# The exponential behind the step's copy, and a query prepared one batch ahead: order of events in a batch loop of attention

## The reference

```python
    x = x + _L0_xattn_ref(ctx_1024, _layernorm(x, axis=-1), mask_BxS2_bk0, ...)
    ...
        xn = layer_norm(x, g1, b1)                      # x here: the context, (16, 1601, 256)
        ln_lat = layer_norm(latents, g2, b2)
        q = ln_lat @ Wq
        kv = jnp.concatenate([xn, ln_lat], axis=1) @ Wkv
        ...                                             # 16 heads of 64
        weight = jnp.einsum('bhld,bhnd->bhln', q * scale, k * scale)
        weight = jnp.where(full_mask[:, None, None, :], weight, neg)
        weight = jax.nn.softmax(weight.astype(jnp.float32), axis=-1).astype(q.dtype)
        out = jnp.einsum('bhln,bhnd->bhld', weight, v)
        return out @ Wout
```

## Time and profile before

| | us |
|---|---|
| median of 3 runs | 1907.46 (1906.87 to 1907.48) |
| the profiled execution's own time | 1906.96 |
| its span in the profile | 1905.2 |
| PE busy | 1805.6 (95%) |
| DVE busy | 1339.1 (70%) |
| ACT busy | 953.3 (50%) |
| POOL busy | 597.4 (31%) |

### The profile page before, as it was taken

One profiled execution on the slowest core, in us unless ns is written; L12 is line 12 of the kernel. 1 busy time (PEld: TensorE's weight loads), 2 busy tenths in 40 slices (PEclk: granted clock), 3 DMA queues, 4 the chain that ended last, 5 costly groups with the idle time before them and its releaser, 6 DMA issues. The chain is left out here.

```text
span 1905.2 us, 32021 instructions
## 1 busy us (share of the span) xinstructions
PE 1805.6 (95%) x10259; PEld 1573.4 (83%) x10259; DVE 1339.1 (70%) x3147; ACT 953.3 (50%) x1665; POOL 597.4 (31%) x647
## 2 busy tenths in 40 slices
PE   5889999999999999999999999999999978888998
PEld 4678888888888888888888888888888877766886
DVE  7577767777777777776767777777777437767666
ACT  4545555554645454555555554645454323334444
POOL 3424344241515151524334241515150013430000
PEclk9989999999999999999999999999999999999999
DMA  7812313131313122222313131313131585502231
GB/s 279 292 54 87 107 45 116 40 110 47 103 47 103 64 89 80 79 88 87 108 42 114 41 109 47 103 47 103 64 108 51 199 351 208 205 2 78 91 116 36
DMA packets 125421, 197.24 MB, mean 104 GB/s; under 512 B 71568, under 2 KB 95024, under 8 KB 119216
## 3 DMA queue, kind: packets, MB, share of 16 engines
q1 hardware_dynamic: 125360, 196.45, 30.8%
HBM read 123.01 MB, written 73.42 MB: 103 GB/s over the span
## 5 line engine op out<-in xcount | busy, mean ns | idle before, releaser
L249 PE MATMUL o_bank<-probT,val 128*128 128x512 f32 x2496 | 684.9, 410 | 7.6 <-DVE probT L888 5.0
L249 PE MATMUL s_bank<-late,fore 128*128 128x416 f32 x3072 | 626.0, 353 | 12.5 <-DVE fore L893 10.3
L249 PEld LDWEIGHTS s_bank<-late,fore 128*128 128x128 f32 x3072 | 570.4, 188 | 42.9 <-issue 11.5
L249 PEld LDWEIGHTS o_bank<-probT,val 128*128 128x128 f32 x2496 | 438.7, 189 | 90.2 <-DVE probT L888 11.6
L852 ACT ACTIVATE prob<-prob,negmax 128x1665 f32<-128x1665 f32 x128 | 216.2, 1689 | 379.2 <-DVE negmax L917 379.2
L888 DVE TENSOR_TENSOR probT<-t_bank,probT 128x512 fp32r<-128x512 f32 x416 | 283.0, 687 | 145.7 <-ACT probT L830 140.8
L830 ACT ACTIVATE probT<-t_bank 128x512 fp32r<-128x512 f32 x416 | 242.8, 591 | 222.4 <-PE t_bank L969 222.2
L912 DVE CUSTOM_DVE_ANT_0 prob<-s_bank,bias 128x416 f32<-128x416 f32 x512 | 295.8, 585 | 67.6 <-PE s_bank L249 66.6
L969 PE MATMUL t_bank<-ident,prob 128*128 128x128 f32 x1664 | 251.0, 274 | 10.5 <-DVE probT L888 6.4
L969 PEld LDWEIGHTS t_bank<-ident,prob 128*128 128x128 f32 x1664 | 205.9, 141 | 51.7 <-DVE probT L888 13.9
L806 POOL TENSOR_TENSOR late_y<-w_raw,late_y 128x1280 fp32r<-128x1280 f32 x16 | 48.1, 3007 | 397.3 <-ACT late_y L824 397.3
(11 more groups left out here) (215 smaller groups left out, 1895.9 us busy)
## 6 DMA issues: line engine op xcount, KB each, us to landing
o_scratch<-outT SPq DMA_DIRECT2D x32, 1024.0 KB, 4.8
stage<-in_ctx SPq DMA_DIRECT2D x48, 512.0 KB, 3.9
w_scratch<-late_y SPq DMA_DIRECT2D x16, 1280.0 KB, 6.5
ffn_w<-o_scratch SPq DMA_DIRECT2D x9, 2048.0 KB, 8.9
qk<-qk_scratch SPq DMA_DIRECT2D x16, 1024.0 KB, 6.8
ffn_w<-w_scratch SPq DMA_DIRECT2D x16, 1024.0 KB, 7.2
late_y<-o_scratch SPq DMA_DIRECT2D x6, 2048.0 KB, 8.1
w_raw<-in_wall SPq DMA_DIRECT2D x16, 640.0 KB, 7.0
```

Source lines behind the costliest of these rows:

```text
L249: mm = pe.matmul(out, weights(a), moving(b), start=first and n == 0, stop=last and n == 2)
```

## The change

The diff moves entries in the lists of events, and nothing else is computed. E i no longer follows A i 3 at once: it is put after the T of the same chunk step (behind Q i+1, and behind what scores of the next pair the step has). Where a step has no T (X of batch 0) it is put after the step's scores. Q 0 of a batch leaves the start of X, except in batch 0, and becomes event G at the end of the Y ahead, behind chunk step 11. Only ACT takes part in E; only ACT and DVE in Q and G. So PE's own order stays as it is.

```diff
 X_AT = {"W": 6, "P3": 10, "N0": 3, "N1": 7, "S4": 6, "S0": 10, "S1": 12}
-Y_AT = {"P7": 9, "N2": 0, ...
+Y_AT = {"P7": 9, "G": 11, "N2": 0, ...
...
-        ev += [("K", 0, 0), ("K", 1, 0), ("Q", 0), ("K", 0, 1), ("K", 1, 1)]
+        ev += [("K", 0, 0), ("K", 1, 0)] + ([] if has_b else [("Q", 0)]) + [("K", 0, 1), ("K", 1, 1)]
...
+            done = [("E", i) for i, j in here if j == 3]
+            if not has_b:
+                ev += done
...
             if c + 2 < CH:
                 ev += [("T", 1, c + 2)]
+            if has_a:
+                ev += done
             ev += [("V", 1, c)]
...
         ev += [("T", 0, c + 2)] if c + 2 < CH else [("T", 2, c - 11)]
+        ev += [("E", i) for i, j in here if j == 3]
         ev += [("V", 0, c)]
...
+        if has_next and c == Y_AT["G"]:
+            ev += [("G",)]
...
-    if j == 3:
-        ev += [("E", i)]
...
-            if ("Q", 0) in x and b.off > 0:
+            if ("K", 0, 0) in x and b.off > 0:
                 F.mask_bias(pool, b)
...
-                if kind == "Q":
+                if kind in "QG":
 
-                    i = e[1]
-                    wait(act, q_in, b, 16, 16)
-                    wait(act, score_out, b, 32, 4 * i - 4)
+                    i, n = (e[1], b) if kind == "Q" else (0, Batch(b.off + 1, b.turn))
+                    wait(act, q_in, n, 16, 16)
+                    wait(act, score_out, n, 32, 4 * i - 4)
```

More of the change, by code:

```diff
@@ L71 @@
 X_AT = {"W": 6, "P3": 10, "N0": 3, "N1": 7, "S4": 6, "S0": 10, "S1": 12}
-Y_AT = {"P7": 9, "N2": 0, "N3": 0, "S2": 3, "S3": 3, "H": (3, 3, 5, 6, 8, 9, 10)}
+Y_AT = {"P7": 9, "G": 11, "N2": 0, "N3": 0, "S2": 3, "S3": 3, "H": (3, 3, 5, 6, 8, 9, 10)}
 H_CHUNKS = ((13, 0, 1), (2, 3), (4, 5), (6, 7), (8, 9), (10, 11), (12,))
@@ L90, in plan_x @@
                 ev += [("K", 0, 3), ("K", 1, 3)]
-            for i, j in units[at:at + X_UNITS[c]]:
+            here = units[at:at + X_UNITS[c]]
+            for i, j in here:
                 ev += unit_events(i, j, 0)
             at += X_UNITS[c]
+            done = [("E", i) for i, j in here if j == 3]
+            if not has_b:
+                ev += done
             if c == X_AT["P3"] and has_b:
@@ L127, in plan_y @@
     for c in range(CH):
-        for i, j in units[at:at + Y_UNITS[c]]:
+        here = units[at:at + Y_UNITS[c]]
+        for i, j in here:
             ev += unit_events(i, j, 4)
@@ L889, in half @@
                                       ALU.subtract).then_inc(t_done, 1)
-                if kind == "Q":
-                    i = e[1]
-                    wait(dve, q_high, b, 8, i + 1)
+                if kind in "QG":
+                    i, n = (e[1], b) if kind == "Q" else (0, Batch(b.off + 1, b.turn))
+                    wait(dve, q_high, n, 8, i + 1)
                     dve.tensor_tensor(qkT[:, i % 2, :, 1, :], qk32[:, i, :, :, :].rearrange("p k h l -> p k (h l)"),
```

## The result

The changed kernel takes 1885.55 us (median of 4, 1884.22 to 1886.81) against 1907.47 before (4 runs): a ratio of 0.9885, 95% interval 0.9873 to 0.9896. That is 21.9 us less; 22 were forecast, and the time lies 0.55 us from the predicted 1885.

What follows compares the result with a forecast made beforehand. PE was taken to bound the kernel, idle 1.30 us a batch. Terms 8.5 + 6.45 + 5.8 + 1.0 = 21.75 us, taken from 1906.96, gave 1885.2, predicted as 1885 us, range 1881 to 1891.

Steps and rivals of the forecast that it cites:

- pair 7's exponential: Near the end of Y: the stall before a transposition goes, 0.51 us in 15 batches, more in batch 0, together 8.5 us.
- pairs 2 and 3: X, step 9: the old stall goes, gaining 0.50 less 0.07 charged at chunk 12, in 15 batches: 6.45 us.
- query 0: Turn into a batch: stall for the query's low part shrinks, 5.8 us with POOL first at the port, otherwise 9.25.
- batch 0: In batch 0's X: pair 2's exponential no longer stands ahead of query 4, and work behind comes earlier: 1.0 us.
- The bound and the stake: Batch loop: PE sets the pace, so the most the change can give is its idle time, 1.30 us a batch.
- Rival 1: In X: pair 2's delay comes back, another 0.43 us a batch is lost, 6.45 less gain, 1891.7 us; chance 0.12.
- Rival 3: End of Y: DVE gets the port before POOL, so query 0 gives 9.25 us, sum 1882; chance 0.2.
- Rival 4: The clock falls, ending within 0.2% of no change; place and chance are not in the text given.

Runs made afterwards that it cites:

- The early split: The changed kernel with query 0 split at step 6 of Y instead of step 11: 1880.71 us.
- pair 7's exponential alone: Against the kernel before, only the exponential of pair 7 moved, in all 16 batches; other exponentials and query 0 stay where they were: 1897.34 us.
- the doubled delay: The changed kernel, but pair 2's exponential of batches 1 to 15 one copy later, behind that of chunk 10: 1919.73 us.
- pair 2 as before: The changed kernel, but pair 2's exponential of batches 1 to 15 back at its old place, right behind its scores: 1881.50 us.

## Why the prediction was right

The mechanisms were right, and the total was closer than its terms. Both kernels issue the same instructions on TensorE in the same order, so their starts can be compared one by one; that puts the gain in the batch loop where it belongs:

| term | worked out | measured |
|---|---|---|
| pair 7's exponential | 8.5 | 9.4 |
| pairs 2 and 3 | 6.45 | 6.2 |
| query 0 | 5.8 | 4.0 |
| batch 0 | 1.0 | 2.6 |
| sum | 21.75 | 22.2 |

Query 0 brought 1.8 us less than was worked out, and batch 0 with pair 7 brought 2.5 more. That these errors nearly cancel is luck.

**The bound and the stake.** Read rightly: TensorE sets the pace, 1.30 us idle a batch was the stake, and 1.14 of it came (89.30 to 88.16).

**Pair 7's exponential, 8.5 us.** The stall is gone as reckoned, in all batches: 0.57 us each in 15 of them (0.51 was worked out) and 0.9 in batch 0. Alone the edit gave more, by the race at batch 1 and the clock in batch 0, neither of which is in this term.

**Pairs 2 and 3, 6.45 us.** The old stall went, the new lateness came exactly where it was put, at chunk 12 behind pair 3's scaling. Its size was 0.14 rather than 0.07 us a batch, and moving pair 2 back gave 0.19. The working also missed that query 4's low part would meet the weights' split of GpSimd and take 0.81 instead of 0.42 us; VectorE waits 1.9 us for the exponential soon after, so it cost nothing. The starts of pair 2's exponential and scaling, counted from the transposition of chunk 9, are within 0.02 us of those worked out: that starts at 720.49 after and 731.12 before, the exponential at +1.13 (worked out: 1.12), the scaling at +3.13 (3.12).

**Query 0, 5.8 us.** The query's low part did lose the port to the centring, by 0.07 us where 0.03 was worked out. With a margin that thin the call was luck as much as reckoning. The stall that stays is 0.45 instead of the 0.36 implied (0.13 and 0.23). The early split shows the parts: 0.25 for the port and 0.20 that stays without it. Over the 15 turns that gave 4.0 us: 1.0 and 1.1 at those into batches 1 and 15, 0.15 to 0.18 at the looped ones (0.27 was worked out), and 0.02 at the one into batch 2, where less was to be had than 0.63, because the loss was 0.50 before.

The Trainium skill's rule ("SBUF — State Buffer", section "Who interferes with whom"), that the one issued first holds the port for its whole length, is borne out by both sides of the race: with GpSimd 0.07 us ahead VectorE's 0.41 us became 2.60, with VectorE 0.08 us ahead (batch 1 of pair 7's exponential alone) it took 0.42 and GpSimd's bias 1.68 instead of 1.48.

**Batch 0, 1.0 us.** The term that was mis-sized most in proportion. Only query 4's stall was counted; the shorter wait for pair 3's scaling came on top. TensorE of the kernel before at the loop's first transposition, that of half 0 and the next batch's first scores; the last line is the changed kernel's first scores.

```profile
82.97 1.94 PE L983 MATMUL s_bank<-ident,stage 128*128 128x128 f32 x16 [2.30 <-PEq L1840]
...
115.38 1.68 PE L969 MATMUL t_bank<-ident,prob 128*128 128x128 f32 x8 [4.04 <-DVE prob L924]
...
166.86 1.39 PE L249 MATMUL s_bank<-late,fore 128*128 128x416 f32 x6 [1.23 <-DVE fore L893]
```

```profile
162.96 1.37 PE L257 MATMUL s_bank<-late,fore 128*128 128x416 f32 x6 [0.17 <-issue]
```

The kernel before takes 32.41 us from the first to the second, the changed one 29.83: 2.58 us. Both ran at the lower clock for some 10 us in this batch, and the gain reaches batch 1 in full. All of batch 0 is 4.50 us shorter (83.89 against 79.39): 2.6 by this order, 0.9 by pair 7's stall, 1.0 at the turn.

**Rivals.** Rival 1 (pair 2's delay comes back) was true in kind and small, 2.9 us at most; the doubled delay shows what it would have cost, and that the slower end was only one copy away. Rival 3 (VectorE wins the port) was open until the run, and missed by 0.07 us. Rival 4 (the clock falls) didn't come: it stayed at 1.00 in the looped batches. Its size was also mis-stated: 21.75 us are 1.5% of the 1432 us of the loop, not 1.2%.

## What to carry to other kernels

An engine that takes part in many short chains should not let a long instruction without urgency stand ahead of a short one that the busiest engine waits for; swapping the two can cost nothing if the long one would have started no earlier anyway. Before moving it, walk the chain behind it up to the next thing that the bound engine asks for: here one swap was free, one cost 0.19 us a batch, and one copy further it cost 2.4. And a low-cost piece moved to an idle place of its engine can land on a shared port; look at what the neighbour does in the same microsecond. Last, check a good forecast term by term: here the sum was right within 3% while one term was 1.8 us too large and another 1.6 too small.

## What the hardware showed

TensorE's granted clock in batch 0 goes with differences of one to two microseconds between kernels that issue the same work there. Windows of 14 us (busy us and instructions of the five engines, granted clock, DMA) of the kernel before, the changed one, pair 2 as before, and pair 2 later still:

```profile
116.00:130.00 14.00, 12.13 (x46) 10.30 (x46) 9.40 (x19) 7.39 (x11) 0.00 (x0) 0.64 0.37 122
```

```profile
116.00:130.00 14.00, 12.69 (x53) 11.06 (x54) 11.44 (x27) 6.91 (x11) 0.71 (x3) 0.73 0.36 122
```

```profile
116.00:130.00 14.00, 12.94 (x59) 11.30 (x60) 12.33 (x30) 6.56 (x10) 1.73 (x4) 0.81 0.36 122
```

```profile
116.00:130.00 14.00, 12.68 (x65) 11.37 (x66) 13.56 (x31) 6.94 (x11) 2.38 (x8) 0.96 0.37 122
```

The last three issue the same instructions in batch 0. Each has the idle time of 2.8 us before the first transposition of half 0, and then a mix of short waits; a part of the stretch runs at 1.2 instead of 2.4 GHz, and how long a part differs between the profiles: the granted clock of the 14 us is 0.73, 0.81 and 0.96. Batch 0 took 79.39, 78.37 and 76.94 us in them. In all ten profiles the clock falls within 1.1 us of that transposition, and nowhere else in the batch loop behind it. So a stall in front of dense work may cost more than its own length. That the stall brings the fall is inferred from this order in time; no kernel here is without the stall, and with one profile each it is open what sets the length. A difference of a microsecond in a kernel like this one should be read off the timeline rather than the total.
